# A one-core AdaLN, quantised FFN, GRU and expert-FFN kernel: where activations are transposed, how weight scales are found, and which PSUM bank the fill uses

## The chip, the cores and the metric

One NeuronCore of a Trainium2 chip runs the whole program. The metric is the device time of one execution in microseconds (us), lower is better. The figure for the kernel before is the median of three runs; beside it stands one profiled execution with its own time.

## The reference

x is [16, 256, 512] (batch, time, width). Everything below is computed in order:

```python
# layer 0, conditioning: block sums of x -> one attention over 8 blocks -> proj [B, 512]
xc = layernorm(x + proj) * gamma + beta
# layer 0, FFN: blocks of 32 share a power-of-two scale (MX quantisation) on both operands
gate, up = mx_linear(xc, w_gate), mx_linear(xc, w_up)      # 512 -> 2048
x = x + mx_linear(silu(gate) * up, w_down)                 # 2048 -> 512
# layer 1, conditioning: a GRU over the 256 time steps, h0 = cond_2048
gi, gh = x_t @ W_ih + b_ih, h @ W_hh + b_hh                # 512 -> 3 * 512
r, z = sigmoid(i_r + h_r), sigmoid(i_z + h_z)
n = tanh(i_n + r * h_n);  h = (1 - z) * n + z * h
# layer 1, FFN on the states hs: base product plus 16 rank-16 experts, the best 2 of 16 by a small router
out = x + hs @ W.T + bias + sum_e coeff_e * (hs @ A_e.T) @ B_e.T
```

## The kernel before

The 4096 rows (256 steps of 16 batch rows) are cut into 32 tiles of 128 rows, that is of 8 GRU steps. Each engine has its program written out by hand, with semaphores between them, so every engine works strictly in its own order.

Three stages follow each other. **The pieces** (0 to about 136 us): 24 weight pieces of 1024 columns are loaded, rounded to the quantised grid and turned into `wq`; beside them x is summed for the attention. **The fill** (about 136 to 244 us) and **the recurrence** are one software pipeline, run over a tile counter c = -4 ... 32 with 8 slots (s = 0 ... 7) each. In the slots of c the kernel does, for five different tiles at once: Q, the normalised and quantised input of tile c+4 (`qx`); F, the FFN of tile c+3; E, its end for tile c+2 (last `down` products, residual `x1`, and `x1T`); I, the GRU input products `x_wih` of tile c+1; R, the 8 recurrence steps of tile c, one a slot; L, the expert FFN of tile c-1. For c < 0 there is no R: that is the fill.

In slot (c, s) TensorE (PE in the profile) first does the 96 small products of the recurrence (L1305: `ps_rn`, then `ps_z`), which need the state `hT` of the slot before, and after them `others`: `gate` (even s, L1131) or `up` (odd s, L1137) of the FFN, transposes, `down` (L1155), `x_wih` (L1198), `base` and `route` (L1207). VectorE (DVE) does the chain of the recurrence from `r_half` (L747) to the low half of `hT` (L733), with other work before, within and after it. So a slot lasts as long as the longer of two things: PE's products of that slot, or the DVE chain that gives the next `hT`.

The FFN goes in four quarters n of 512 columns. For one quarter: `gate` into `ps_gate`, silu by ScalarE (ACT) into `gs`, `up` into the same bank (`ps_gate = ps_up`), `inter` = product by DVE (L827), block maxima, 8-bit value `f8`, clip `f8c` (L812), `qf` by GpSimd (POOL, L1020). Then `turn_inter` transposes `qf` with four PE transposes into PSUM (L1146), ACT copies it to `qfT` (L510), and `down` reads it a slot later. `qx` is turned once a tile in the same way (`turn_qx` L1186, copy L536 into `qxT`). PE does `turn_inter` in slots 0, 2, 4 and 6 and `turn_qx` in slot 7.

The GRU and expert weights are kept as two f16 parts with a power-of-two scale, from the largest absolute value. DVE finds these: for W_hh at (-3, 0) (`chunk_max`, L698), for W_ih at (-2, 0) (L662) and for WL (L667). W_ih is loaded into `wih` chunk by chunk once W_hh's parts have been taken from there: SP waits for `whh_lo` at (-3, 6). SP issues nearly all the DMAs, in order. In the fill `ps_z` lies idle.

## Time and profile before

| | us |
|---|---|
| median of 3 runs | 1749.04 (1748.38 to 1749.63) |
| the profiled execution's own time | 1750.32 |
| its span in the trace | 1748.5 |
| PE busy | 1585.6 (91%) |
| DVE busy | 1417.0 (81%) |
| ACT busy | 710.7 (41%) |
| POOL busy | 498.4 (29%) |
| DMA queue of the kernel's own transfers | 75.03 MB, 12.6% of 16 engines |

The span runs from 0; the pieces end at about 136 us, the first recurrence step starts at 244.4 us and the last at 1729.2 us. A busy share is the mean over stages with different limits, so it has to be read stage by stage; rows of the trace give start, duration, engine and line of one instruction or of a run of equal ones, and in brackets how long its engine had been idle and who ended that.

### The profile page before, as it was taken

How to read it: one execution, taken by the hardware profiler on the slowest of the kernel's cores; microseconds unless marked ns; L12 is line 12 of the kernel's file. 1: busy time of each engine (PE TensorE's matmuls, PEld its weight loads, DVE VectorE, ACT ScalarE, POOL GpSimd, SP SyncE). 2: the span in 40 equal slices, each digit the busy share in tenths (PEclk: the TensorE clock that was granted, in tenths of full speed). 3: DMA queues.
4: the chain of work that ended last, by engine and by line, in shares of the span. 5: the costliest groups of instructions: out<-in, count | busy, mean ns of one | idle time of the engine just before them, and what ended most of it. 6: DMA issues, size and time to landing. Idle time of an engine off the chain costs nothing.

```text
span 1748.5 us, 76340 instructions
## 1 busy us (share of the span) xinstructions
PE 1585.6 (91%) x32908; PEld 1240.8 (71%) x32908; DVE 1417.0 (81%) x5579; ACT 710.7 (41%) x1760; POOL 498.4 (29%) x573
## 2 busy tenths in 40 slices
PE   5534489999999999999999999999999999999986
PEld 2221167777787877778777777877777777778874
DVE  7898888888888888888888888888888888887654
ACT  5653244444444344434344434443443444443331
POOL 6773232222222222222222222222222222221100
PEclk9855699999999999999999999999999999999998
DMA  7733100011001010001111000110100010000000
GB/s 246 265 141 111 43 26 27 34 33 33 13 29 33 33 33 33 29 31 34 33 33 34 33 26 16 33 33 33 33 33 27 33 33 33 27 27 27 21 15 20
DMA packets 35408, 80.09 MB, mean 46 GB/s; under 512 B 4864, under 2 KB 5248, under 8 KB 34688
## 3 DMA queue, kind: packets, MB, share of 16 engines
q1 hardware_dynamic: 34784, 75.03, 12.6%
q8 instruction: 259, 4.24, 1.1%
q14 instruction: 77, 0.63, 0.1%
q10 hardware_dynamic: 288, 0.19, 0.0%
HBM read 58.43 MB, written 16.78 MB: 43 GB/s over the span
## 4 chain that ended last, share of the span: by engine, by line
PE 76%; DVE 16%; issue 2%; DMA 2%; POOL 2%; ACT 1%; DVEq 0%; ACTq 0%; POOLq 0%; SPq 0%
PE ps_rn_turn L1305 23%; PE ps_gi L1198 11%; PE ps_z L1305 10%; PE ps_gate_up L1137 6%; PE ps_down L1155 6%; PE ps_gate_up L1131 4%; PE ps_base L1207 4%; PE ps_base L1251 3%; PE ps_route L1207 3%; DVE fe L795 1%; PE ps_rn_turn L1146 1%; PE ps_rn_turn L1175 1%; DVE gi L595 1%; DVE gi L593 1%; DVE zn L780 1%
## 5 line engine op out<-in xcount | busy, mean ns | idle before, releaser
L1305 PE MATMUL ps_rn_turn<-hT,whh 128*128 128x32 f16 x16320 | 449.2, 176 | 39.2 <-DVE hT L733 38.8
L1305 PEld LDWEIGHTS ps_rn_turn<-hT,whh 128*128 128x128 f16 x16320 | 435.0, 96 | 65.7 <-DVE hT L733 58.2
L1020 POOL TENSOR_TENSOR qf<-f8c,fe 128x512 bf16<-128x512 bf16 x128 | 135.6, 1059 | 892.4 <-DVE f8c L812 872.8
L1198 PE MATMUL ps_gi<-x1T,wih 128*128 128x128 f16 x4608 | 288.6, 219 | 1.2 <-ACT gi L544 1.2
L1198 PEld LDWEIGHTS ps_gi<-x1T,wih 128*128 128x128 f16 x4608 | 270.3, 98 | 25.6 <-issue 1.5
L553 ACT ACTIVATE r_tanh<-r_pre,scale_half 128x64 f32<-128x64 f32 x256 | 89.0, 348 | 461.5 <-DVE r_pre L753 461.5
L1305 PE MATMUL ps_z<-hT,whh 128*128 128x32 f16 x8160 | 243.3, 176 | 0.0
L1305 PEld LDWEIGHTS ps_z<-hT,whh 128*128 128x128 f16 x8160 | 222.7, 96 | 0.0
L544 ACT ACTIVATE gi<-ps_gi,b_i,scale_x 128x128 f32<-128x128 f32 x384 | 144.7, 457 | 181.9 <-PE ps_gi L1198 181.9
L747 DVE TENSOR_TENSOR r_half<-ps_rn_turn,gi 128x64 f32<-128x64 f32 x256 | 56.6, 221 | 137.6 <-PE ps_rn_turn L1305 134.4
L555 ACT ACTIVATE z_tanh<-z_pre,scale_half 128x64 f32<-128x64 f32 x256 | 89.0, 348 | 157.9 <-DVE z_pre L763 157.9
L1131 PE MATMUL ps_gate_up<-wq,qxT 128*128 128x512 bf16 x512 | 135.5, 388 | 12.8 <-DVE inter L827 12.8
L1137 PE MATMUL ps_gate_up<-wq,qxT 128*128 128x512 bf16 x512 | 139.1, 396 | 2.4 <-ACT sg_gs L504 2.4
L1155 PE MATMUL ps_down<-wq,qfT 128*128 128x512 bf16 x512 | 134.4, 386 | 0.0
L557 ACT ACTIVATE n<-n_pre,scale_half 128x64 f32<-128x64 f32 x256 | 89.0, 348 | 20.6 <-DVE n_pre L770 10.5
L1207 PE MATMUL ps_base<-wl,hT 128*128 128x512 f16 x384 | 94.3, 382 | 0.0
L827 DVE TENSOR_TENSOR inter<-ps_gate_up,sg_gs 128x512 f32<-128x512 f32 x128 | 87.4, 683 | 7.1 <-PE ps_gate_up L1137 7.1
L504 ACT ACTIVATE sg_gs<-ps_gate_up 128x512 f32<-128x512 f32 x128 | 74.2, 580 | 44.5 <-PE ps_gate_up L1131 44.5
L788 DVE TENSOR_REDUCE fam<-inter 128x16 f32<-128x512 f32 x128 | 87.9, 686 | 4.4
L806 DVE SCALAR_TENSOR_TENSOR f<-inter,finv 128x512 fp8e4<-128x512 f32 x128 | 87.7, 685 | 0.0
L1155 PEld LDWEIGHTS ps_down<-wq,qfT 128*128 128x128 bf16 x512 | 48.6, 100 | 49.9 <-issue 4.6
L1137 PEld LDWEIGHTS ps_gate_up<-wq,qxT 128*128 128x128 bf16 x512 | 43.3, 99 | 55.6 <-issue 20.9
(197 smaller groups left out, 2590.1 us busy)
## 6 DMA issues: line engine op xcount, KB each, us to landing
wih<-in_x_steps SPq DMA_DIRECT2D x32, 256.0 KB, 5.4
xin<-in_x_steps SPq DMA_DIRECT2D x32, 256.0 KB, 3.5
xres<-in_x_steps SPq DMA_DIRECT2D x32, 256.0 KB, 3.1
x_dram<-x SPq DMA_DIRECT2D x32, 256.0 KB, 2.1
x_in<-x_dram SPq DMA_DIRECT2D x32, 256.0 KB, 2.8
out_rows<-y SPq DMA_DIRECT2D x32, 256.0 KB, 2.0
wst<-in_ffn_w SPq DMA_DIRECT2D x12, 512.0 KB, 3.7
sg_gs<-in_ffn_w SPq DMA_DIRECT2D x12, 512.0 KB, 3.9
```

Of the source, the lines that this page charges most:

```text
L544: last = nc.scalar.activation(gi_gate(i, g)[:, k, :], ps_gi[:, k * P:(k + 1) * P], ACT.Identity, bias=b_i[:, g * KD + k:g * KD + k + 1], s ...
L553: nc.scalar.activation(r_tanh[:, :], r_pre[:, :], ACT.Tanh, scale=HALF_S_INV).then_inc(r_ok, 1)
L555: nc.scalar.activation(z_tanh[:, :], z_pre[:, :], ACT.Tanh, scale=HALF_S_INV).then_inc(z_ok, 1)
L557: nc.scalar.activation(n[:, :], n_pre[:, :], ACT.Tanh, scale=HALF_S_INV).then_inc(n_ok, 1)
L788: v.tensor_reduce(am[:, :], blocked(src[:, :]), AX_X, ALU.max, apply_absolute_value=True).then_inc(small, 1)
L1020: g.tensor_tensor(blocked(qf[:, :]), blocked(f8c[:, :]), spread(fe16[:, :]), ALU.mult).then_inc(qf_done, 1)
L1131: last = mm(ps_gate[:, :], qxT[:, k, :], w_ffn(0, n, k), start=k == 0, stop=k == KD - 1)
L1137: last = mm(ps_up[:, :], qxT[:, k, :], w_ffn(8, n, k), start=k == 0, stop=k == KD - 1)
L1155: last = mm(ps_down[:, :], qfT[:, i, :], w_down(i), start=i == 0, stop=i == NF * KD - 1)
L1198: last = mm(ps_gi[:, j * P:(j + 1) * P], wih_parts[:, k, at:at + P], x1T[:, x, k, :], start=k + w + x == 0, stop=k == KD - 1 and w == 1)
L1207: last = mm(out, hT[l % 2][:, 2 * k + x, :], wl_parts[:, k, begin:begin + n], start=k + w + x == 0, stop=stop and w == 1)
L1305: last = mm(ps[:, (at + j) * 2 * B:(at + j + 1) * 2 * B], whh[:, k, u, gate * D + j * P:gate * D + (j + 1) * P], hx(t)[:, 2 * k:2 * k + 2, ...
```

## The change

1. `qx` and `qf` are no longer turned by PE and copied by ACT. SP issues `dma_start_transpose` from `qx` to `qxT` and from `qf` to `qfT`, in slots 7 and 1, 3, 5, 7. `qxT` has two buffers. POOL writes `qf` or `qx` again once that DMA has landed; `gate` and `down` wait for the landing.
2. The scales of W_hh, W_ih and WL come from row sums of absolute values, by ACT (`absolute_sums`), instead of maxima by DVE: W_hh's beside the last four pieces, W_ih's in slots 4 and 5 of c = -3, WL's in 6 and 7. In c = -3 and -2 ACT's `weights` come after `others`.
3. W_ih is loaded at (-3, 0), once the last piece is out, into tiles that are free by then (`wih_staged`: `gi` and the new `stage`); BT is loaded at (-1, 0).
4. The first 11 `up` products (`FILL_UPS`) go to `ps_z`, and `gs` has two buffers. `up` then waits for `inter` of the quarter before instead of silu, and `gate` no longer waits for `inter`.

The diff without its context lines and without the lists of semaphores; it is indented less:

```diff
@@ -67,6 +67,7 @@
+FILL_UPS = 11
@@ -114,8 +115,6 @@
-turn_b = ps_turn[:, :].bitcast(BF16)
-turn_q = ps_route[:, :].bitcast(BF16)
@@ -123,11 +122,12 @@
-wih, wl = sb("wih", [P, KD + 1, GATES]), sb("wl", [P, KD + 1, D + ROUTE])
+wih, wl = sb("wih", [P, KD, GATES]), sb("wl", [P, KD + 1, D + ROUTE])
-bt = sb("bt", [P, XA // P, D])
+stage = sb("stage", [P, 2 * GATES])
+bt = stage[:, 2 * PIECE:3 * PIECE].rearrange("p (m n) -> p m n", m=XA // P)
@@ -155,10 +155,10 @@
-qxT = sb("qxT", [P, KD, P], BF16)
+qxT = [sb(f"qxT{u}", [P, KD, P], BF16) for u in range(2)]
-gs, inter = sg_gs[:, D:2 * D], sb("inter", [P, D])
+gs, inter = [sg_gs[:, u * D:(u + 1) * D] for u in range(2)], sb("inter", [P, D])
@@ -179,7 +179,8 @@
-x1_in, x1_bias, y = sb("x1_in", [P, D]), sb("x1_bias", [P, D]), sb("y", [P, D])
+x1_in_bias, y = sb("x1_in_bias", [P, 2 * D]), sb("y", [P, D])
+x1_in, x1_bias = x1_in_bias[:, 0:D], x1_in_bias[:, D:2 * D]
@@ -191,10 +192,11 @@
-wst = [sb("wst0", [P, PIECE]), sg_gs[:, 0:PIECE]]
+wst = [stage[:, 0:PIECE], sg_gs[:, 0:PIECE]]
+wih_staged = [x[:, u * GATES:(u + 1) * GATES] for x in (gi, stage) for u in range(2)]
-w_abs = [sb(f"w_abs{u}", [P, PIECE], U8)[:, :] for u in range(2)]
+w_abs = [stage[:, PIECE + u * PIECE // 4:PIECE + (u + 1) * PIECE // 4].bitcast(U8) for u in range(2)]
@@ -215,7 +217,8 @@
-chunk_max, most = sb("chunk_max", [P, KD]), sb("most", [P, 2])
+row_sums, most = sb("row_sums", [P, 3, KD]), sb("most", [P, 2])
+unused = x1_in_bias[:, :].bitcast(BF16)
@@ -282,6 +285,10 @@
+def up_bank(i):
+    return ps_z if i < FILL_UPS else ps_up
@@ -378,16 +385,38 @@
+    def turn_qx(q):
+        sp.wait_ge(qx_done, count(q, 1, 1))
+        wait(sp, up_mm, count(q - 1, NF))
+        sp.dma_start_transpose(qxT[q % 2][:, :, :], qx[:, :]).then_inc(qx_turned[q % 2], 16)
+    def turn_inter(f, n):
+        sp.wait_ge(qf_done, count(f, NF, n + 1))
+        wait(sp, d_mm, count(f - 1, NF, n + 1))
+        sp.dma_start_transpose(qfT[:, n * KD:(n + 1) * KD, :], qf[:, :]).then_inc(qf_turned[n], 16)
+    def turns(c, s):
+        Q, F, E, I, R, L = stages(c)
+        if E and s == 1:
+            turn_inter(c + 2, NF - 1)
+        if Q and s == 7:
+            turn_qx(c + 4)
+        if F and s in (3, 5, 7):
+            turn_inter(c + 3, s // 2 - 1)
+        turns(c, s)
-        if c == -3 and s == STEPS - 2:
+        if (c, s) == (-3, 0):
+            sp.wait_ge(w_out, PIECES)
+            for k in range(KD):
+                sp.dma_start(wih_staged[k], W_ih[:, k, :]).then_inc(wih_loaded, 16)
-            for k in range(KD):
-                sp.wait_ge(whh_lo, min(k + 2, KD))
-                sp.dma_start(wih[:, k + 1, :], W_ih[:, k, :]).then_inc(wih_loaded, 16)
+        if (c, s) == (-1, 0):
+            sp.wait_ge(wih_lo, KD)
@@ -466,8 +495,21 @@
+    def absolute_sums(which, k, w):
+        wait(act, summed_w, which * KD + k)
+        nc.scalar.activation(unused[:, 0:w.shape[1]], w, ACT.Abs,
+                             accum_out=row_sums[:, which, k:k + 1]).then_inc(summed_w, 1)
+        if c == -3 and s in (4, 5):
+            for k in (2 * s - 8, 2 * s - 7):
+                act.wait_ge(wih_loaded, 16 * KD)
+                absolute_sums(1, k, wih_staged[k])
+        if c == -3 and s in (6, 7):
+            for k in (2 * s - 12, 2 * s - 11):
+                act.wait_ge(wl_loaded, 16)
+                absolute_sums(2, k, wl[:, k + 1, :])
@@ -481,8 +523,8 @@
-            wait(act, wih_lo, k)
-            nc.scalar.activation(wih_parts[:, k, 0:GATES], wih[:, k + 1, :], ACT.Copy,
+            act.wait_ge(whh_lo, KD)
+            nc.scalar.activation(wih_parts[:, k, 0:GATES], wih_staged[k], ACT.Copy,
@@ -500,16 +542,9 @@
-            wait(act, inter_done, count(f, NF, s // 2))
-            nc.scalar.activation(gs, ps_gate[:, :], ACT.Silu, scale=SHRUNK / W_GREW).then_inc(gs_done, 1)
-        for t, n, there in ((f, s // 2 - 2, F and s in (4, 6)), (e, s // 2 + 2, E and s in (0, 2))):
-            if there:
-                act.wait_ge(t_mm, count(t, NF, n + 1))
-                if n == 0:
-                    wait(act, d_mm, count(t, NF))
-                nc.scalar.activation(qfT[:, n * KD:(n + 1) * KD, :],
-                                     turn_b[:, 0:D].rearrange("p (k n) -> p k n", k=KD),
-                                     ACT.Copy).then_inc(t_ev, 1)
+            at = count(f, NF, s // 2)
+            wait(act, inter_done, at - 1)
+            nc.scalar.activation(gs[at % 2], ps_gate[:, :], ACT.Silu, scale=SHRUNK / W_GREW).then_inc(gs_done, 1)
@@ -530,11 +565,6 @@
-        if Q and s == 7:
-            act.wait_ge(q_mm, count(c + 4, 1, 1))
-            wait(act, up_mm, count(c + 4, NF))
-            nc.scalar.activation(qxT[:, :, :], turn_q[:, 0:D].rearrange("p (k n) -> p k n", k=KD),
-                                 ACT.Copy).then_inc(q_ev, 1)
@@ -555,13 +585,18 @@
-        if c in (-3, -2, 0):
+        if c == 0:
+        if c in (-3, -2):
+            weights(c, s)
+        if p >= PIECES - KD:
+            act.wait_ge(whh_loaded, 16 * KD)
+            absolute_sums(0, p - PIECES + KD, wih[:, p - PIECES + KD, :])
@@ -655,17 +690,12 @@
-        at = 2 * KD + 9
+        at = 9
-            for k in range(KD):
-                dve.wait_ge(wih_loaded, 16 * KD)
-                v.tensor_reduce(chunk_max[:, k:k + 1], wih[:, k + 1, :], AX_X, ALU.max,
-                                apply_absolute_value=True).then_inc(most_dve, 1)
-            dve.wait_ge(most_dve, at)
-            v.reduce_max(most[:, 0:1], chunk_max[:, :], AX_X).then_inc(most_dve, 1)
-            dve.wait_ge(wl_loaded, 16)
-            v.tensor_reduce(most[:, 1:2], wl[:, 1:KD + 1, :].rearrange("p k n -> p (k n)"), AX_X, ALU.max,
-                            apply_absolute_value=True).then_inc(most_dve, 1)
+            dve.wait_ge(most_mm, 1)
+            dve.wait_ge(summed_w, 3 * KD)
+            for i in range(2):
+                v.reduce_max(most[:, i:i + 1], row_sums[:, i + 1, :], AX_X).then_inc(most_dve, 1)
@@ -681,7 +711,7 @@
-            v.scalar_tensor_tensor(wih_parts[:, k, GATES:2 * GATES], wih[:, k + 1, :], S_I,
+            v.scalar_tensor_tensor(wih_parts[:, k, GATES:2 * GATES], wih_staged[k], S_I,
@@ -693,21 +723,17 @@
-            for k in range(KD):
-                dve.wait_ge(whh_loaded, 16 * KD)
-                v.tensor_reduce(chunk_max[:, k:k + 1], wih[:, k, :], AX_X, ALU.max,
-                                apply_absolute_value=True).then_inc(most_dve, 1)
-            dve.wait_ge(most_dve, KD)
-            v.reduce_max(most[:, 0:1], chunk_max[:, :], AX_X).then_inc(most_dve, 1)
+            dve.wait_ge(summed_w, KD)
+            v.reduce_max(most[:, 0:1], row_sums[:, 0, :], AX_X).then_inc(most_dve, 1)
-            scales_in_row(s, KD + 2, least, scale_row)
+            scales_in_row(s, 2, least, scale_row)
-            dve.wait_ge(most_dve, KD + 8)
+            dve.wait_ge(most_dve, 8)
@@ -824,7 +850,7 @@
-                v.tensor_tensor(inter[:, :], ps_up[:, :], gs, ALU.mult).then_inc(inter_done, 1)
+                v.tensor_tensor(inter[:, :], up_bank(at)[:, :], gs[at % 2], ALU.mult).then_inc(inter_done, 1)
@@ -1016,7 +1042,7 @@
-                wait(pool, t_mm, at)
+                wait(pool, qf_turned[(at - 1) % NF], (at + NF - 1) // NF * 16)
@@ -1048,7 +1074,7 @@
-            wait(pool, q_mm, count(q, 1))
+            wait(pool, qx_turned[(q - 1) % 2], (q + 1) // 2 * 16)
@@ -1125,29 +1151,27 @@
-            pe.wait_ge(q_ev, count(f, 1, 1))
-        wait(pe, inter_done, count(f, NF, n))
+            pe.wait_ge(qx_turned[f % 2], (f // 2 + 1) * 16)
+        i = count(f, NF, n)
+        wait(pe, gs_done, i)
+        if i > FILL_UPS:
+            pe.wait_ge(inter_done, i)
-            last = mm(ps_gate[:, :], qxT[:, k, :], w_ffn(0, n, k), start=k == 0, stop=k == KD - 1)
+            last = mm(ps_gate[:, :], qxT[f % 2][:, k, :], w_ffn(0, n, k), start=k == 0, stop=k == KD - 1)
-        pe.wait_ge(gs_done, count(f, NF, n + 1))
+        i = count(f, NF, n)
+        if i < FILL_UPS:
+            wait(pe, inter_done, i)
+        else:
+            pe.wait_ge(gs_done, i + 1)
-            last = mm(ps_up[:, :], qxT[:, k, :], w_ffn(8, n, k), start=k == 0, stop=k == KD - 1)
+            last = mm(up_bank(i)[:, :], qxT[f % 2][:, k, :], w_ffn(8, n, k), start=k == 0, stop=k == KD - 1)
-    def turn_inter(f, n):
-        pe.wait_ge(qf_done, count(f, NF, n + 1))
-        if n == 2:
-            wait(pe, x_ev, count(f, 1))
-        wait(pe, t_ev, count(f, NF, n))
-        for k in range(KD):
-            last = turn_(turn_b[:, k * P:(k + 1) * P], qf[:, k * P:(k + 1) * P], idb[:, :])
-        last.then_inc(t_mm, 1)
-        pe.wait_ge(t_ev, count(f, NF, n + 1))
+        pe.wait_ge(qf_turned[n], (f + 1) * 16)
@@ -1170,21 +1194,11 @@
-        pe.wait_ge(t_ev, count(e + 1, NF, 2))
+        pe.wait_ge(x1_done, count(e, 1, 1))
+        wait(pe, x_ev, count(e, 1))
-    def turn_qx(q, E, L):
-        pe.wait_ge(qx_done, count(q, 1, 1))
-        wait(pe, q_ev, count(q, 1))
-        if E:
-            pe.wait_ge(x_scale_ok, count(q - 2, 1, 1))
-        elif L:
-            pe.wait_ge(wxaT_ok, count(q - 5, 1, 1))
-        for k in range(KD):
-            last = turn_(turn_q[:, k * P:(k + 1) * P], qx[:, k * P:(k + 1) * P], idb[:, :])
-        last.then_inc(q_mm, 1)
@@ -1213,7 +1227,6 @@
-            wait(pe, q_ev, count(l + 4, 1, 1))
@@ -1276,10 +1289,6 @@
-        if E and s in (0, 2):
-            turn_inter(e, s // 2 + 2)
-        if F and s in (4, 6):
-            turn_inter(f, s // 2 - 2)
@@ -1288,8 +1297,6 @@
-        if Q and s == 7:
-            turn_qx(c + 4, E, L)
@@ -1310,10 +1317,9 @@
-        at = (c + 3) * (KD + 9)
+        at = 0 if c == -3 else 9
-            pe.wait_ge(most_dve, at + KD + 2)
-            pe.wait_ge(q_ev, c + 4)
+            pe.wait_ge(most_dve, at + 2)
@@ -1321,7 +1327,7 @@
-            pe.wait_ge(most_dve, KD + 9 if c == -3 else 2 * KD + 20)
+            pe.wait_ge(most_dve, 9 if c == -3 else 20)
@@ -1337,6 +1343,8 @@
+        if (c, s) == (-1, 7):
+            pe.wait_ge(inter_done, FILL_UPS)
```

## Rows read from the trace of the kernel before

**Rows 1.** The page, part 4: the chain that ended last, shares by engine.
```profile
PE 76%; DVE 16%; issue 2%; DMA 2%; POOL 2%; ACT 1%; DVEq 0%; ACTq 0%; POOLq 0%; SPq 0%
```

**Rows 2.** Tile hT: recurrence group, then min/median/max ns, first and last start.
```profile
L1305 PE MATMUL ps_rn_turn<-hT,whh x16320: 176/176/210, 249.5 to 1730.8; 128*128 128x32 f16 x200
```

**Rows 3.** Timeline of PE: starts of slots 7, 0, 1, 3, 5, 0.
```profile
709.98 1.75 PE L1305 MATMUL ps_rn_turn<-hT,whh 128*128 128x32 f16 x64
...
716.78 1.75 PE L1305 MATMUL ps_rn_turn<-hT,whh 128*128 128x32 f16 x64
...
722.57 1.78 PE L1305 MATMUL ps_rn_turn<-hT,whh 128*128 128x32 f16 x64
...
734.43 1.77 PE L1305 MATMUL ps_rn_turn<-hT,whh 128*128 128x32 f16 x64 [0.59 <-DVE hT L733]
...
745.81 1.75 PE L1305 MATMUL ps_rn_turn<-hT,whh 128*128 128x32 f16 x64
...
763.97 1.75 PE L1305 MATMUL ps_rn_turn<-hT,whh 128*128 128x32 f16 x64
```

**Rows 4.** Timeline of DVE, same stretch: ends of chains, and one slow small operation.
```profile
709.20 0.22 DVE L733 TENSOR_TENSOR hT<-h,hT 128x64 f16<-128x64 f32 x1
...
714.59 0.23 DVE L733 TENSOR_TENSOR hT<-h,hT 128x64 f16<-128x64 f32 x1
...
721.58 0.22 DVE L733 TENSOR_TENSOR hT<-h,hT 128x64 f16<-128x64 f32 x1
...
731.07 0.88 DVE L795 TENSOR_SCALAR fe<-fam 128x16 f32<-128x16 f32 x1
...
745.48 0.22 DVE L733 TENSOR_TENSOR hT<-h,hT 128x64 f16<-128x64 f32 x1
```

**Rows 5.** The chain of waits, in order of time: start, us, group.
```profile
716.72 0.22 PE ps_route L1186 x4
...
720.21 0.22 PE ps_rn_turn L1146 x4
```

**Rows 6.** Timeline of POOL: two quarters of qf in a steady tile.
```profile
700.34 1.05 POOL L1020 TENSOR_TENSOR qf<-f8c,fe 128x512 bf16<-128x512 bf16 x1 [9.67 <-DVE f8c L812]
...
710.64 1.05 POOL L1020 TENSOR_TENSOR qf<-f8c,fe 128x512 bf16<-128x512 bf16 x1 [4.76 <-DVE f8c L812]
```

**Rows 7.** The DMA view: issues by tile, KB each, median us to landing.
```profile
wih<-in_x_steps SPq DMA_DIRECT2D x32, 256.0 KB, 5.4
...
out_rows<-y SPq DMA_DIRECT2D x32, 256.0 KB, 2.0
...
beta_b<-in_beta SPq DMA_DIRECT2D x1, 256.0 KB, 8.8
```

**Rows 8.** Timeline of DVE in the fill.
```profile
136.13 6.72 DVE L698 TENSOR_REDUCE chunk_max<-wih 128x1 f32<-128x1536 f32 x4
...
148.79 0.69 DVE L827 TENSOR_TENSOR inter<-ps_gate_up,sg_gs 128x512 f32<-128x512 f32 x1 [2.94 <-PE ps_gate_up L1137]
...
176.23 6.73 DVE L662 TENSOR_REDUCE chunk_max<-wih 128x1 f32<-128x1536 f32 x4 [2.45 <-DMA wih<-in_W_ih]
...
183.07 3.61 DVE L667 TENSOR_REDUCE most<-wl 128x1 f32<-128x3328 f32 x1
...
231.18 0.69 DVE L827 TENSOR_TENSOR inter<-ps_gate_up,sg_gs 128x512 f32<-128x512 f32 x1 [0.79 <-PE ps_gate_up L1137]
...
237.84 0.69 DVE L827 TENSOR_TENSOR inter<-ps_gate_up,sg_gs 128x512 f32<-128x512 f32 x1 [0.72 <-PE ps_gate_up L1137]
```

**Rows 9.** Timeline of POOL in the fill: the first qx.
```profile
136.29 1.05 POOL L1052 TENSOR_TENSOR qx<-q8c,qe 128x512 bf16<-128x512 bf16 x1 [1.50 <-DVE q8c L812]
```

**Rows 10.** Timeline of PE in the fill: the first gate, and the first recurrence step.
```profile
144.22 1.89 PE L1131 MATMUL ps_gate_up<-wq,qxT 128*128 128x512 bf16 x4
...
244.42 1.75 PE L1305 MATMUL ps_rn_turn<-hx_first,whh 128*128 128x32 f16 x64
```

**Rows 11.** Timeline of ACT in the fill: two copies of 1536 columns.
```profile
151.96 3.03 ACT L480 ACTIVATE whh<-wih,scale 128x1536 f16<-128x1536 f32 x2
```

6 lines of the change are left out of this document (3 added, 3 removed).

## The prediction

> **What bounds the kernel now.** I read the chain of waits first: of the chain that ended last, PE has 76% and DVE 16% [rows 1]. That is a mean over stages, so the next view is the timeline by stage. Recurrence steps follow each other from 244.42 us on [rows 10], and their last group starts at 1730.8 [rows 2]; before that lie the pieces and the fill.
>
> *Recurrence.* A tile of 8 slots takes 763.97 - 716.78 = 47.19 us [rows 3]. For each slot the reader compares two rows: when `hT` is complete (start plus duration of L733) and when PE starts the next slot's products. If PE starts later, PE's own work sets the slot and the difference is DVE's slack. If PE shows idle time ended by `hT`, the DVE chain sets it. Slack before slot 7: 709.98 - 709.42 = 0.56; before slot 0: 716.78 - 714.82 = 1.96; before slot 1: 722.57 - 721.80 = 0.77; before slot 5: 745.81 - 745.70 = 0.11, of which about 0.05 is the signal's way. Slot 3 begins after 0.59 us of idleness that `hT` ended [rows 3, 4]. So six or seven of the eight slots are PE's, and slot 2 is DVE's: its chain holds a `fe` of 0.88 us on 16 columns [rows 4].
>
> *Fill.* DVE works nearly without a gap, and two blocks stand out: 6.72 us of W_hh maxima, and 2.45 us waiting for W_ih followed by 6.73 and 3.61 us of maxima [rows 8].
>
> **The change, part by part.**
>
> *Turns in the recurrence.* Each group of four PE transposes takes 0.22 us of the chain [rows 5]. A tile loses five: slots 0, 2, 4, 6 and 7, 1.10 us of PE. What remains of each is read from the slack behind it:
> - slot 0: slack 0.77 is more than 0.22, so 0.22 is kept.
> - slot 2: PE already waits 0.59, so 0.
> - slot 4: only 0.11 - 0.05 = 0.06 can be kept; then `hT` is late, and DVE goes on without a gap into slot 5, so perhaps nothing.
> - slot 6: slack 0.56, 0.22 kept. Slot 7: slack 1.96, 0.22 kept.
>
> Sum 0.66 to 0.72; I take 0.70. F and Q both run beside the recurrence in c = 0 to 27, 28 tiles: **19.6 us**. The ACT copies that go were never waited for by the chain of `hT` beyond 1% [rows 1]; I give them 0.
>
> *What takes the turns' place.* A DMA must land before `down` (two slots later, about 12 us) and before POOL writes the single `qf` again. The tighter one is `qf`: its shortest gap is 710.64 - 701.39 = 9.25 us [rows 6]. No row shows a transposing DMA. The nearest are plain DMAs of 256 KB, twice these bytes: 2.0, 5.4 and 8.8 us from issue to landing [rows 7]. I take 5.4, the slower of the two that occur 32 times, because a transpose of 2-byte elements should go worse than a copy; both ends stay for the range. All three are below 9.25, so it is hidden in the recurrence, at cost 0. If that cover is gone, the price is in the last rival.
>
> SP waits in order, so each `turn_inter` holds up what is queued behind it. In slot 7 that is the store of x1 and of y, which waits for `y` of the same slot anyway; in slot 3 the load of `xin`, which POOL needs only in the next tile. Cost 0.
>
> The Trainium skill speaks against this part. VectorE: DVE Perf Modes, section The three transpose paths, gives a 128x128 bf16 transpose as 390 ns on TensorE and 1309 ns by DMA, and its rules say to use TensorE where PSUM will do. The trace has PE at 0.22 us for four. By the page four blocks by DMA would be 5.2 us, an estimate; hidden or not decides, and the sum would stay as it is.
>
> *Start of the fill.* The block of 6.72 leaves DVE. In its place ACT does four sums of 1536 columns between the last pieces, 3.03 / 2 = 1.5 us each by its copies [rows 11], and an activation with a sum may take a little more. ACT is in the round of the pieces (DVE waits for its squares), and it has 1 to 3.5 us free in each: I let one of the four delay the last pieces, 1.5 us. The first `qx` is then ready at 136.29 + 1.05 + 1.5 = 138.8 [rows 9], and with 5.4 for its DMA the first `gate` starts at 144.2, where it starts now, 144.22 [rows 10]. So **the 6.7 us buy nothing by themselves**: the wait for the maxima is replaced by a wait for a DMA. With 2.0 it would be 3.4 us earlier, with 8.8 3.4 later. The free bank gives the first `up` the 0.7 us for which it waited on silu, and in c = -3 ACT's sums before the W_hh copies cost DVE about as much (0.8). Together **0**.
>
> *Middle of the fill.* W_ih is issued about 23 us earlier and has long landed; ACT's eight sums (4 x 1.5 for W_ih, 4 x about 0.9 for WL by width) fit into c = -3 by about 168 us, before DVE needs them. Gone are 2.45 + 6.73 + 3.61 = 12.8 us [rows 8], come are two maxima over four columns, 0.3: **12.5 us**. Since all behind hangs on DVE's order, it passes through.
>
> *End of the fill, c = -1.* DVE waits twice for `up`, 0.79 and 0.72 [rows 8]. `gate` no longer waits for `inter` and a turn is gone, PE comes some 1.7 us earlier, and DVE becomes the bound: 1.5, plus the last turn before the first step, 0.2: **1.7 us**. The pairs of quarters are only 6 to 7 us apart here; DMAs beyond about 6 us would take this back.
>
> *Sum.* 19.6 + 0 + 12.5 + 1.7 = 33.8 us. Against the profiled execution: span 1748.5 - 33.8 = 1714.7, its own time 1750.3 - 33.8 = 1716.5. It stood 1.3 us above the median, so the median becomes 1749.0 - 33.8 = **1715.2 us**. Bounds of the unknown costs: the first landing +-3.4, later ones up to +3, ACT beside the pieces -1.5 to +3 (none or all but one delayed), slot 4 +-1.
>
> **Rivals.**
> 1. *PE's time isn't given back in the recurrence.* DVE, busy 81%, becomes the bound in more slots than I read, or `qf` and `hT` shift so that other small operations get as slow as the `fe` of 0.88. For it: slack of 0.11 before slot 5. Against: 0.56 to 1.96 elsewhere. Then only the fill gains, 14.2 us: 1735.
> 2. *More comes.* Transposes land in 2 us (3.4 earlier at the start, another 1 to 2 in c = -3), and slots 2 and 4 keep their 0.22 too because ACT without its copies shortens DVE's chain: 28 x 1.10 = 30.8 instead of 19.6. Both: 1749.0 - 30.8 - 14.2 - 4 = 1700.
> 3. *Slower: the DMA takes longer than the gap.* `qf` is one buffer: write (1.05), signal (about 0.4), DMA, next write. Once the DMA needs L, a tile takes at least 4 x (1.45 + L). It reaches 47.19 at L = 10.3; from L = 10.5 the loss over 29 tiles eats the 14.2 us of the fill, and at L = 12 a tile is 53.8, which is 29 x 6.6 = 191 us more: about 1926. For it: a landing of 8.8 for a DMA with nothing to transpose, and five such DMAs a tile in one queue. Against: half the bytes, and DMA engines nearly idle here.
> 4. *It doesn't do what it says*: PE is not the bound and the fill is bound by something that the removed blocks hid; within 0.2% of before. Rows 3 and 8 speak against it.
>
> **How the numbers follow.** Forecast (about 1706 to 1726) 0.60; rival 1 0.17; rival 2 0.12; rival 3 0.08; rival 4 0.03. The range leaves out rivals 3 and 4 and the far part of 2: 1702 to 1736. Faster 0.60 + 0.17 + 0.12 = 0.89; within 0.2% (3.5 us, about what a measurement of this kernel can tell from no change) 0.03; slower 0.08.
>
> **What would show it.** Tile period about 46.5 us instead of 47.19, with PE idle before slot 3 near 0.8 and a first idle before slot 5. Landings of the transposing DMAs between 2 and 9 us, and POOL's `qf` still released by DVE's `f8c`, not by a DMA. First `gate` near 144, released by a DMA. No DVE wait or maxima around 176; the first recurrence step near 230. Wrong would make it: a DMA as what POOL or `down` waits for in the recurrence, ACT stretching the last pieces by more than 3 us, or tables reloaded by ACT between its sums and silu.

## The result, and the profile after

The changed kernel takes 1716.51 us (median of four runs, 1716.04 to 1720.65) against 1749.34 (1748.38 to 1751.13) for the kernel before: ratio 0.9814, 95% interval 0.9802 to 0.9826. Predicted were 1715.2 us, in a range of 1702 to 1736. Inside the sum, though, the landing of the DMA and the free bank had a wrong size, and a new wait in the fill was missed. In the experiments "the changed kernel" is this one; on another chip it took 1717.86 us.

The profiled execution was the longest of the four, 1720.65 us, with a span of 1718.8: it lies 4.1 us above the forecast for a profiled execution (1716.5), where the median lies 1.3 above its own. Where its 29.7 us against the span before came from, by the starts of DVE's `inter` (the product of silu and up; they are numbered from 0), of the first recurrence step and of the last:

| stretch | before | after | difference | predicted |
|---|---|---|---|---|
| to inter 0: pieces, start of the fill | 148.79 | 146.17 | -2.6 | 0 |
| inter 0 to inter 6: middle of the fill | 62.30 | 48.76 | -13.5 | -12.5 |
| inter 6 to inter 7 | 9.44 | 12.26 | +2.8 | 0 |
| inter 7 to the first step | 23.89 | 22.77 | -1.1 | -1.7 |
| first step to the start of the last | 1484.8 | 1469.2 | -15.6 | -19.6 |
| behind it | 19.3 | 19.6 | +0.3 | 0 |

The page of the changed kernel, lines of its parts 1, 3 and 4: busy time, the DMA queue of the kernel's own transfers, and the chain that ended last by engine (before: [rows 1]).

```profile
PE 1556.5 (91%) x32268; PEld 1204.4 (70%) x32268; DVE 1393.3 (81%) x5571; ACT 644.6 (38%) x1624; POOL 497.5 (29%) x573
...
q1 hardware_dynamic: 121824, 96.02, 20.9%
...
PE 76%; DVE 15%; issue 3%; ACT 2%; DMA 2%; POOL 2%; SPq 0%; DVEq 0%; ACTq 0%; POOLq 0%
```

PE lost 29 us of work and DVE 24, and the queue moved 96 MB instead of 75, in 121824 packets instead of 34784. The shares of the chain are nearly the same as before: they don't tell where the gain is. The timeline does.

**Recurrence.** PE of the changed kernel, starts of slots 7, 0, 1, 3, 5, 0 and of the last slot of all (before: [rows 3]):

```profile
690.69 1.75 PE L1312 MATMUL ps_rn_turn<-hT,whh 128*128 128x32 f16 x64
697.26 1.75 PE L1312 MATMUL ps_rn_turn<-hT,whh 128*128 128x32 f16 x64
702.83 1.77 PE L1312 MATMUL ps_rn_turn<-hT,whh 128*128 128x32 f16 x64
...
714.69 1.76 PE L1312 MATMUL ps_rn_turn<-hT,whh 128*128 128x32 f16 x64 [0.81 <-DVE hT L759]
...
726.01 1.77 PE L1312 MATMUL ps_rn_turn<-hT,whh 128*128 128x32 f16 x64
...
728.53 0.22 PE L1187 MATMUL ps_route<-idb,row_power 128*1 128x128 bf16 x1
...
743.75 1.75 PE L1312 MATMUL ps_rn_turn<-hT,whh 128*128 128x32 f16 x64
...
1699.18 1.75 PE L1312 MATMUL ps_rn_turn<-hT,whh 128*128 128x32 f16 x64
```

DVE beside it (before: [rows 4]), the transposing DMAs in the view of DMA issues (last number: median us to landing), and POOL's `qf` ([rows 6]):

```profile
711.32 0.88 DVE L821 TENSOR_SCALAR fe<-fam 128x16 f32<-128x16 f32 x1
...
725.73 0.22 DVE L759 TENSOR_TENSOR hT<-h,hT 128x64 f16<-128x64 f32 x1
...
728.32 0.16 DVE L910 TENSOR_SCALAR row_power<-row_max 128x1 uint16<-128x1 uint16 x1
```
```profile
qfT<-qf SPq DMA_TRANSPOSE x128, 2.5
...
qxT<-qx SPq DMA_TRANSPOSE x32, 2.9
```
```profile
715.84 1.05 POOL L1046 TENSOR_TENSOR qf<-f8c,fe 128x512 bf16<-128x512 bf16 x1 [3.67 <-DVE f8c L838]
```

A tile takes 743.75 - 697.26 = 46.49 us, 0.70 less. Slots 6, 7 and 0 became 0.22, 0.23 and 0.23 shorter (medians of 27 tiles), slot 4 by 0.06. Slot 2 is DVE's still: PE's wait ahead of slot 3 grew from 0.59 to 0.81 and took what the missing turn gave. In slot 5, longer by 0.04, PE now comes so early that its one small product on `row_power` waits for DVE: 728.32 + 0.16 is 728.48, and it starts at 728.53. POOL's `qf` waits for DVE's `f8c` in all 128 cases, never for a transpose, which lands in 2.5 us (median) and not in the 5.4 of the prediction.

**Start of the fill.** DVE, PE and SP of the changed kernel:

```profile
140.98 0.16 DVE L727 TENSOR_REDUCE most<-row_sums 128x1 f32<-128x4 f32 x1 [2.29 <-ACT x_in_bias L500]
...
146.17 0.69 DVE L853 TENSOR_TENSOR inter<-ps_z,sg_gs 128x512 f32<-128x512 f32 x1 [2.17 <-PE ps_z L1170]
```
```profile
141.41 1.01 PE L1326 MATMUL ps_route<-idf,most 128*1 128x128 f32 x4 [2.98 <-DVE most L729]
142.43 1.89 PE L1160 MATMUL ps_gate_up<-wq,qxT 128*128 128x512 bf16 x4
```
```profile
139.85 1.31 SPq L391 DMA_TRANSPOSE qxT<-qx  x1
```

And a row of the kernel before, PE, which the prediction had not read; it stands just ahead of its first gate in [rows 10]:

```profile
143.27 1.01 PE L1320 MATMUL ps_route<-idf,most 128*1 128x128 f32 x4 [5.27 <-DVE most L703]
```

The turn of `most` comes before the first gate in PE's order. Before, PE stood idle for 5.27 us ahead of it, for DVE's maxima. In the changed kernel two things end within 0.04 us of each other: the DMA of `qx`, issued at 139.85, lands at 142.38, and the turn of `most`, for which PE waits 2.98 us because DVE waits 2.29 for ACT's fourth sum, ends at 142.42. The gate starts at 142.43.

How much of the 2.6 us is the change's needs more than these two traces. The eleven traces of kernels with the sums beside the pieces start `q8c`, DVE's last step before the first `qx`, anywhere from 132.99 to 138.85 us (the changed kernel: 138.27 and 137.69), the three without them at 135.56 to 136.28. Behind `q8c` the traces agree: from there to inter 0 it takes 12.8 to 13.0 us in the three kernels with W_hh's maxima on DVE, and 7.5 to 8.2 in the ten with the sums and two banks. So about 5 us are gained behind the pieces, and this execution lost 2.5 of them ahead of it.

**Middle and end of the fill.** DVE of the changed kernel, and ACT at its second wait (before: [rows 8]):

```profile
177.67 0.69 DVE L853 TENSOR_TENSOR inter<-ps_z,sg_gs 128x512 f32<-128x512 f32 x1 [2.62 <-PE ps_z L1170]
...
199.66 1.82 DVE L714 SCALAR_TENSOR_TENSOR wih<-stage,scale_l,wih 128x1536 f16<-128x1536 f32 x1 [2.73 <-ACT wih L527]
...
206.52 0.75 DVE L955 SCALAR_TENSOR_TENSOR x1T<-ps_rn_turn,scale_x,x1T 128x512 f16<-128x512 f32 x1 [3.68 <-ACT x1T L566]
...
223.60 0.69 DVE L853 TENSOR_TENSOR inter<-ps_z,sg_gs 128x512 f32<-128x512 f32 x1 [0.72 <-PE ps_z L1170]
```
```profile
197.49 0.60 ACT L547 ACTIVATE sg_gs<-ps_gate_up 128x512 f32<-128x512 f32 x1 [11.05 <-PE ps_gate_up L1160]
197.98 1.56 ACT L527 ACTIVATE wih<-stage,scale_l 128x1536 f16<-128x1536 f32 x1
```

The blocks of [rows 8] at 176 and 183 us are gone. In their place stands a new wait of 2.73 us: the fourth high part of W_ih stands in ACT's order behind a silu, which waits for a gate, and DVE waits for the high part. Of the two waits for `up` in c = -1, 0.79 and 0.72, one is gone and one is left. The first step starts at 229.96 instead of 244.42, 14.5 us earlier.

### The profile page after: what moved, and what is told of

It is laid out like the page before. It is cut to its first block, busy times and chain, and to the rows that moved or that the text cites. A ratio compares the mean times of both kernels' runs of the same rounds, so it can differ in the third digit from the quotient of the medians.

```text
span 1718.8 us, 75109 instructions
## 1 busy us (share of the span) xinstructions
PE 1556.5 (91%) x32268; PEld 1204.4 (70%) x32268; DVE 1393.3 (81%) x5571; ACT 644.6 (38%) x1624; POOL 497.5 (29%) x573
## 3 DMA queue, kind: packets, MB, share of 16 engines
q1 hardware_dynamic: 121824, 96.02, 20.9%
## 4 chain that ended last, share of the span: by engine, by line
PE 76%; DVE 15%; issue 3%; ACT 2%; DMA 2%; POOL 2%; SPq 0%; DVEq 0%; ACTq 0%; POOLq 0%
PE ps_rn_turn L1312 24%; PE ps_gi L1212 12%; PE ps_z L1312 10%; PE ps_down L1179 6%; PE ps_gate_up L1170 6%; PE ps_base L1221 4%; PE ps_gate_up L1160 4%; PE ps_base L1264 3%; PE ps_route L1221 3%; DVE fe L821 1%; POOL qfT L1028 1%; DVE gi L630 1%; DVE gi L628 1%; PE ps_rn_turn L1200 1%; DVE zn L806 1%
## 5 line engine op out<-in xcount | busy, mean ns | idle before, releaser
L1212 PEld LDWEIGHTS ps_gi<-x1T,wih 128*128 128x128 f16 x4608 | 274.5, 98 | 38.2 <-issue 3.8
L1179 PE MATMUL ps_down<-wq,qfT 128*128 128x512 bf16 x512 | 138.0, 394 | 0.0
L1160 PE MATMUL ps_gate_up<-wq,qxT 128*128 128x512 bf16 x512 | 133.0, 382 | 0.0
L1170 PE MATMUL ps_gate_up<-wq,qxT 128*128 128x512 bf16 x468 | 123.6, 387 | 0.5 <-ACT sg_gs L547 0.5
L587 ACT ACTIVATE n<-n_pre,scale_half 128x64 f32<-128x64 f32 x256 | 89.0, 348 | 21.0 <-DVE n_pre L796 11.2
L853 DVE TENSOR_TENSOR inter<-ps_gate_up,sg_gs 128x512 f32<-128x512 f32 x117 | 79.7, 681 | 0.0
L1056 POOL TENSOR_TENSOR xg<-xn,gamma_b 128x512 f32<-128x512 f32 x32 | 40.8, 1276 | 119.2 <-DVE xn L936 119.2
```

The source lines that it names most:

```text
L587: nc.scalar.activation(n[:, :], n_pre[:, :], ACT.Tanh, scale=HALF_S_INV).then_inc(n_ok, 1)
L1160: last = mm(ps_gate[:, :], qxT[f % 2][:, k, :], w_ffn(0, n, k), start=k == 0, stop=k == KD - 1)
L1170: last = mm(up_bank(i)[:, :], qxT[f % 2][:, k, :], w_ffn(8, n, k), start=k == 0, stop=k == KD - 1)
L1179: last = mm(ps_down[:, :], qfT[:, i, :], w_down(i), start=i == 0, stop=i == NF * KD - 1)
L1212: last = mm(ps_gi[:, j * P:(j + 1) * P], wih_parts[:, k, at:at + P], x1T[:, x, k, :], start=k + w + x == 0, stop=k == KD - 1 and w == 1)
```

## Experiments

Each kernel differs from the changed kernel by the edit shown, unless its text says otherwise. A ratio is to runs of the kernel before on the same chip.

### One part of the change undone, or done alone

**The turns back on PE** (loads, sums and the bank stay as changed):

```diff
-            def turn_qx(q):
...
-                sp.dma_start_transpose(qxT[q % 2][:, :, :], qx[:, :]).then_inc(qx_turned[q % 2], 16)
...
+            def turn_inter(f, n):
+                pe.wait_ge(qf_done, count(f, NF, n + 1))
...
+                for k in range(KD):
+                    last = turn_(turn_b[:, k * P:(k + 1) * P], qf[:, k * P:(k + 1) * P], idb[:, :])
```

> The changed kernel with part 1 undone: PE turns qx and qf again and ACT copies them, everything else stays changed. My theory: the turns are worth 0.71 us a tile in 28 tiles of the recurrence, 19.9 us, and nothing in the fill but the last turn, 0.2. So 1716.5 + 20.1 = 1736.6 us, tile period 47.19, first recurrence step about 230.2 us. Rival (the gain is mostly the fill's, and the turns gave back what they saved): 1717 to 1722 us.

**The turns alone** (the kernel before, with its turns by DMA and nothing else of the change):

```diff
+            def turn_inter(f, n):
...
+                sp.dma_start_transpose(qfT[:, n * KD:(n + 1) * KD, :], qf[:, :]).then_inc(qf_turned[n], 16)
...
-                for k in range(KD):
-                    last = turn_(turn_b[:, k * P:(k + 1) * P], qf[:, k * P:(k + 1) * P], idb[:, :])
```

> The kernel before with part 1 alone: qx and qf turned by DMA, maxima by DVE, W_ih late, one bank. My theory: the parts add, so 1749.3 - 20.1 = 1729.2 us, tile period 46.48, first step at about 244.2 us. Rival (the parts need each other: without the second bank the DMA landing shows in the fill, 2.5 us for each of the 12 quarters of the fill): 1729 + up to 20 us.

With PE's turns: 1738.43 us, ratio 0.9943 (0.9928 to 0.9958), 1.8 us above the expectation, which the interval of 5 us does not tell apart. The turns alone: 1738.34 us, ratio 0.9936 (0.9921 to 0.9951), that is 9 us slower than expected, a miss. The tile period is as expected in both, 47.19 and 46.49 us. In the fill both lose. From inter 0 to the first step it takes 88.35 us with PE's turns (changed kernel 83.79), and 99.73 with the turns alone (before 95.63). With PE's turns that does not show in the first step, 229.07 for 230.2 expected, because inter 0 came at 140.72, 5.4 us before that of the changed kernel; 5.3 of these lie before `q8c`, that is before anything is turned. DVE and ACT with PE's turns:

```profile
153.14 1.82 DVE L746 SCALAR_TENSOR_TENSOR whh<-wih,scale,whh 128x1536 f16<-128x1536 f32 x1 [1.14 <-ACT whh L504]
```
```profile
147.91 0.60 ACT L535 ACTIVATE qfT<-ps_rn_turn 128x512 bf16<-128x512 bf16 x1 [3.58 <-PE ps_rn_turn L1174]
```

ACT's copies of the turned quarters share its order with the eight sums and the high parts of W_hh, and DVE waits for these three times, 1.14, 1.05 and 0.86 us. DVE and SP with the turns alone:

```profile
182.81 6.74 DVE L667 TENSOR_REDUCE chunk_max<-wih 128x1 f32<-128x1536 f32 x4 [8.49 <-DMA wih<-in_W_ih]
```
```profile
166.72 1.20 SPq L387 DMA_TRANSPOSE qfT<-qf  x1
...
168.59 2.76 SPq L408 DMA_DIRECT2D wih<-in_W_ih  x4
```

SP waits in order. It stands in the turn of a quarter until 166.72, so the late load of W_ih, issued at 161.82 before, is issued at 168.59, and DVE waits for it for 8.49 us where it waited for 2.45 [rows 8]; from the first issue to the last landing the four loads take 14.2 us here and 14.4 before. The early load takes W_ih out of that place. So the parts don't add: 10.4 us for the turns alone, 10.3 for all the rest, 32 for both. Of the 11 us between, the stretch from inter 0 to the first step holds 8.6 (4.1 lost with the turns alone, 7.3 gained by the rest, 11.8 by both). The others aren't assigned: the pieces alone differ by several us from one execution to the next.

**One bank in the fill:**

```diff
-FILL_UPS = 11
+FILL_UPS = 0
...
-                    pe.wait_ge(inter_done, FILL_UPS)
+                    wait(pe, inter_done, FILL_UPS)
```

> The changed kernel itself again, unaltered, as the measure for the three kernels run beside it on the same chip. Expected 1716.5 us, 32 to 33 us under the kernel before (ratio 0.981). Also asked of it: whether its recurrence again holds slots at the half clock. The profiled execution of the changed kernel had six such slots, some 7.6 us in all, where the kernel before had three; if they come with the turn's removal (a longer wait of TensorE ahead of slot 3, 0.82 us where it was 0.59), this execution has some again, in other steps; if they were an accident of that one execution, it has as few as the kernel before.

> The changed kernel without the last part of the change: the up products go to the one bank in the fill as everywhere else. Two theories. Mine: in the fill, gate and up of the next piece no longer run ahead of the product of the two, so each of the eleven turns in which VectorE waits for silu and up loses its own start-up again (a wait of 0.6 to 0.8 us per turn where it is exposed, some four of them); 1719 us, 2 to 3 us above the changed kernel. The rival: the second bank hides behind VectorE, which is the bound of the middle of the fill, and taking it away costs nothing (1716.5). A third: the products of gate and up queue behind the late product in order and the loss runs on from turn to turn, up to 0.8 x 11 = 9 us (1725).

The changed kernel again: 1717.86 us, ratio 0.9814 (0.9794 to 0.9834). With one bank: 1729.06 us, ratio 0.9881 (0.9865 to 0.9897). All three theories missed: it is 11.2 us, and not in small waits turn by turn. DVE and ACT with one bank:

```profile
163.37 1.82 DVE L751 SCALAR_TENSOR_TENSOR whh<-wih,scale,whh 128x1536 f16<-128x1536 f32 x1 [5.70 <-ACT whh L522]
...
176.82 1.82 DVE L751 SCALAR_TENSOR_TENSOR whh<-wih,scale,whh 128x1536 f16<-128x1536 f32 x1 [4.88 <-ACT whh L522]
```
```profile
158.14 0.60 ACT L547 ACTIVATE sg_gs<-ps_gate_up 128x512 f32<-128x512 f32 x1 [6.67 <-PE ps_gate_up L1160]
158.64 1.48 ACT L500 ACTIVATE x_in_bias<-gi 128x1536 bf16<-128x1536 f32 x1
160.01 0.19 ACT L500 ACTIVATION_READ_ACCUMULATOR x_in_bias<-gi 128x1 f32 x1
...
161.78 1.56 ACT L522 ACTIVATE whh<-wih,scale 128x1536 f16<-128x1536 f32 x1
```

It is a ring of three engines. The next gate waits for `inter`, which in one bank must have been read. ACT's silu waits for that gate; behind the silu stand two sums and the high part; DVE waits for the high part, and its next `inter` stands behind. With two banks the gate, and with it silu and all that is behind it, runs ahead of `inter`, and the sums lie in time that DVE needs anyway. In this order of ACT, its work for the weights is cheap only because of the bank. DVE waits 11.6 us in three waits for W_hh's high parts with one bank, and 0.79 us in one with two. The change puts two things behind silu, the sums and the high parts themselves (`weights` after `others`); no run has one bank without the one or the other, so how the 11.2 us divide between them is open.

**W_hh's maxima back on DVE, no sums beside the last pieces:**

```diff
-                if p >= PIECES - KD:
-                    act.wait_ge(whh_loaded, 16 * KD)
-                    absolute_sums(0, p - PIECES + KD, wih[:, p - PIECES + KD, :])
...
+                    for k in range(KD):
...
+                        v.tensor_reduce(row_sums[:, 0, k:k + 1], wih[:, k, :], AX_X, ALU.max,
+                                        apply_absolute_value=True).then_inc(summed_w, 1)
...
                     v.reduce_max(most[:, 0:1], row_sums[:, 0, :], AX_X)
```

> The changed kernel with the four maxima of W_hh's rows taken by VectorE at the start of the fill, as in the kernel before (6.7 us there), and no sums of them on ScalarE beside the last four pieces. It computes the scales of W_hh from maxima as the kernel before does. My theory, that the 6.7 us taken from VectorE at this place buy next to nothing because the first gate product waits for something else: VectorE's start of the fill comes 1.5 us earlier without ScalarE's sums in the pieces, then takes 6.7 us more, and the first gate moves by 0 to 2.5 us; 1716 to 1719 us. The rival, that VectorE sets the start of the fill by then and all of it returns: 1716.5 + 6.7 - 1.5 - 2.3 (its wait for the fourth sum) = 1719.4 at the least and 1723 at the most.

1717.71 us, ratio 0.9816 (0.9801 to 0.9832): no difference to the changed kernel beside it. Its trace is not the same, though. DVE and PE:

```profile
135.90 6.72 DVE L725 TENSOR_REDUCE row_sums<-wih 128x1 f32<-128x1536 f32 x4
```
```profile
143.09 1.01 PE L1327 MATMUL ps_route<-idf,most 128*1 128x128 f32 x4 [7.37 <-DVE most L730]
144.03 1.89 PE L1161 MATMUL ps_gate_up<-wq,qxT 128*128 128x512 bf16 x4
```

Against the changed kernel in its own execution on this chip, `q8c` comes 2.1 us earlier (135.56 for 137.69), the maxima 2.25 later, the first gate 2.2 later (144.03 for 141.85), inter 0 2.8 later and the first step 3.05 later. Here the DMA of `qx` has landed more than 4 us before the gate, so the maxima alone hold it. In these two executions 1.3 us of it came back in the recurrence and 1.5 behind it, by slots at the half clock (below) and a tail that was not followed further. From `q8c` to inter 0 it takes 12.80 us for 7.89: that is what moving W_hh's maxima takes out of the fill. What ACT's four sums cost beside the pieces in return, 1.5 us by the prediction, isn't settled: 2.1 by this pair, 0.7 in the mean of all the traces, and kernels that are the same up to there differ by 4.5 us. So 3 to 4 us remain by the rows, and the times, with intervals of 5 and 7 us, neither show nor exclude it.

**W_ih's and WL's maxima back on DVE, the load still early:**

```diff
-                    for k in (2 * s - 8, 2 * s - 7):
...
-                        absolute_sums(1, k, wih_staged[k])
...
+                    for which, ws in ((1, wih_staged), (2, [wl[:, k + 1, :] for k in range(KD)])):
+                        for k in range(KD):
+                            v.tensor_reduce(row_sums[:, which, k:k + 1], ws[k], AX_X, ALU.max,
+                                            apply_absolute_value=True).then_inc(summed_w, 1)
```

> The changed kernel with the maxima of W_ih and WL back on VectorE in the second stage of the fill (6.7 + 3.6 us as in the kernel before), while W_ih is still loaded early. The scales of these weights come from maxima again. It tells apart how much of the middle of the fill came from the early load and how much from VectorE's relief. My theory: the 10.3 us return nearly in full, because VectorE is the bound there; less 0.3 us for the maxima of the sums and less up to 2.5 us in which VectorE waits anyway (for x1T 3.7 us, for the high parts 2.7 us): +7.5 to +10 us, 1724 to 1727 us. The rival, the early load alone was worth it and VectorE's work hides in its waits: 1717 to 1720 us.

1726.41 us, ratio 0.9872 (0.9856 to 0.9889), against 0.9814: 0.0058 x 1749 = 10.1 us. My theory held at its upper end, the rival fell. DVE:

```profile
169.43 3.40 DVE L692 TENSOR_REDUCE row_sums<-gi 128x1 f32<-128x1536 f32 x2
172.75 3.40 DVE L692 TENSOR_REDUCE row_sums<-stage 128x1 f32<-128x1536 f32 x2
176.07 3.79 DVE L692 TENSOR_REDUCE row_sums<-wl 128x1 f32<-128x832 f32 x4
```

10.4 us of DVE work (169.43 to 179.86) without a wait ahead of it, and the stretch from inter 0 to the first step is 93.99 us, 10.2 more than in the changed kernel. The middle of the fill is DVE's, and its work there counts in full.

### How slow a transpose may be

Further transposes of the same quarter go ahead of the real one, each waited for. REPEAT is 3, 4 and 5:

```diff
...
+                for r, spare in enumerate(scratch):
+                    sp.dma_start_transpose(spare[:, :, :], qf[:, :]).then_inc(qf_turned[n], 16)
+                    sp.wait_ge(qf_turned[n], (f * REPEAT + r + 1) * 16)
                 sp.dma_start_transpose(qfT[:, n * KD:(n + 1) * KD, :], qf[:, :]).then_inc(qf_turned[n], 16)
...
```

> The changed kernel with each transpose of a quarter made long: two further transposing DMAs of the same data into unused tiles go ahead of the real one, each waited for by the queue before the next is issued. They add work and leave none out. One transpose lands 2.5 us after its issue, so three in a chain take about 3 x 2.6 = 7.8 us. The theory of the prediction (rival 3): beside the recurrence a transpose is free until 4 x (1.45 + L) passes the length of a tile, that is up to L of 10.2; at 7.8 the tile period stays at 46.5 us. In the fill quarters follow each other in as little as 4.7 us, and there a gap of 1.45 + 7.8 = 9.3 us for each of ten makes it 15 to 20 us longer: about 1735 us in all. The rival: the slack of the two-slot distance is smaller than that and the period already grows, by 1 us or more (1765 us and above).

> The same with three further transposes ahead of the real one: L about 4 x 2.6 = 10.4 us, right at the point from which the prediction's rival 3 becomes decisive. By its formula, 4 x (1.45 + 10.4) = 47.4 us a tile, 0.9 more than 46.5; over 29 tiles 26 us, and the fill longer by 30 us: about 1772 us. If the shortest of the four gaps (10.3 us from one qf to the next) can't be made up by the three longer ones, the period is 46.5 + (11.9 - 10.3) = 48.1 us and the time 1794 us.

> The same with four further transposes: L about 13 us. By the formula of the prediction's rival 3 a tile takes 4 x (1.45 + 13) = 57.8 us, 11.3 more than 46.5, over 29 tiles 328 us, and the fill 45 us more: about 2090 us. If the tile period stays near 47 the formula is wrong and the transposes overlap in some way that I don't see.

One execution each. Three: 1735.6 us, tile period 46.48 us, the stretch from inter 0 to the first step 19.8 us longer than in the changed kernel: as expected, and the period can't tell it from one transpose, though 8 of the `qf` of the recurrence already wait for the DMA. Four: 1913.0 us, mean period 51.6 (expected 47.4 to 48.1). Five: 2248.7 us, mean period 62.5 (expected 57.8). POOL with three, and with four:

```profile
709.58 1.05 POOL L1051 TENSOR_TENSOR qf<-f8c,fe 128x512 bf16<-128x512 bf16 x1 [4.72 <-DVE f8c L843]
```
```profile
717.12 1.05 POOL L1051 TENSOR_TENSOR qf<-f8c,fe 128x512 bf16<-128x512 bf16 x1 [10.62 <-DMA qfT<-qf]
```

With four, POOL waits for the DMA in 127 of 128 cases, as rival 3 said. Both terms of the formula 4 x (1.45 + L) can be read in the traces. From the end of a `qf` to the landing of the last link it takes 8.9 us in the mean with three, 11.7 with four and 14.4 with five, over the tiles of the recurrence: 2.9 us a link and not the 2.6 that I had put in, because a link lands 2.5 us after its issue in the median but part of them need 3 to 4. And write and signals take 1.05 + 0.03 + 0.13 = 1.21 us, not 1.45. 4 x (1.21 + 11.68) = 51.6 is the period that was measured; the miss is L, too small by 1.3 and 1.4 us, less 0.24 for the signals. The mean granted clock is lower too, 0.929 with four and 0.960 in the changed kernel, but with POOL's quarters following each other by the DMA alone it does not set the period.

### Two additions

**ACT's high parts of W_ih ahead of its other work in c = -2**, against the new wait of 2.73 us:

```diff
-                if c == 0:
+                if c in (-2, 0):
                     weights(c, s)
                 others(c, s, Q, F, E, I, L)
-                if c in (-3, -2):
+                if c == -3:
                     weights(c, s)
```

> The changed kernel, but ACT does the high parts of W_ih in c = -2 ahead of its other work of the slot, as before the change; c = -3 stays changed. In the changed kernel the fourth high part comes behind a silu that waits for a gate which waits for DVE's row_power, and DVE idles 2.73 us for it. My theory: these 2.7 us lie on the path to the first step, so 1713.8 us and first step near 227.3. Rival: DVE only comes to its next wait (x1T, 3.68 us) earlier and waits longer there: 1716.5 us.

1711.39 us, ratio 0.9792 (0.9779 to 0.9806). The wait is gone, and from inter 0 to the first step it takes 81.08 us for 83.79: 2.7 less, as expected. The other 2.4 us under the 1713.8 is not from the edit by any row I found: in this execution inter 0 came at 143.84 for 146.17, and the recurrence, whose code and slots are the same, held fewer slots at the half clock.

**`xn` one place earlier on DVE beside the recurrence**, against the `fe` of 0.88 us:

```diff
-                if Q and here == (2, 0):
+                if Q and here == ((1, 3) if c >= 0 else (2, 0)):
```

> The changed kernel, with DVE's xn (one operation of 0.54 us) moved ahead of inter and its maxima, for c >= 0, so that POOL's two xg run 1.3 us earlier and are done before DVE's fe of slot 2. My theory: fe of 0.88 us is slow because POOL's xg runs beside it; alone it takes 0.17. Slot 2 is the one slot that DVE sets, so it falls from 5.69 to about 4.98: 28 x 0.7 = 19.6 us, 1697 us, and PE's idle before slot 3 falls from 0.82 to about 0.1. Rival (the slow fe has another cause, or the slowness moves to the next small operation of the same chain): 1716 us, tile period 46.48.

1696.76 us, ratio 0.9695 (0.9679 to 0.9712). The theory held: slot 2 takes 4.97 us for 5.69, a tile 45.78. POOL and DVE of the changed kernel, then of this one:

```profile
710.90 1.27 POOL L1058 TENSOR_TENSOR xg<-xg,beta_b 128x512 f32<-128x512 f32 x1
```
```profile
700.59 1.28 POOL L1058 TENSOR_TENSOR xg<-xg,beta_b 128x512 f32<-128x512 f32 x1
```
```profile
702.33 0.17 DVE L821 TENSOR_SCALAR fe<-fam 128x16 f32<-128x16 f32 x1
```

In the changed kernel `fe` (711.32 to 712.20) lies beside POOL's `xg` (710.90 to 712.17) and ends with it. Here `xg` has ended at 701.87 before `fe` starts, and `fe` takes 0.17. The Trainium skill, SBUF — State Buffer, section SBUF: two separate sides, says of the port pair that VectorE and GpSimd share that whoever starts first holds it for its whole instruction and the other is blocked; of VectorE's operations it names those in a 2-port mode and those with two inputs in SBUF. The rows agree: `fe` starts 0.42 us behind `xg` and ends 0.03 us behind it, and so it is in all 27 tiles from the second on. An operation that reads PSUM isn't slowed: this one of the changed kernel lies beside the same `xg` and takes what it takes elsewhere:

```profile
711.19 0.21 DVE L782 TENSOR_TENSOR hn<-ps_rn_turn,hn_half 128x64 f32<-128x64 f32 x1
```

**Both:**

> Both of my additions in one kernel: ScalarE's weight work ahead of the other work in the fill's second stage, and the normalised x one place earlier on VectorE beside the recurrence. Alone the second gave 1696.8 us, and the first took 2.7 us from the stretch between the first product of silu and up and the first step of the recurrence. They touch different stretches, so they should add: 1696.8 - 2.7 = 1694 us (ratio 0.969 to the kernel before). If the fill's gain was an accident of how early its pieces ran, this gives 1696.8 again.

1693.18 us, ratio 0.9685 (0.9666 to 0.9703), 0.8 us from the expectation. From inter 0 to the first step 81.01 us, a tile 45.79: each part is where it was alone. It has the lowest median of the kernels here; its interval overlaps that of `xn` alone.

## Why the prediction was right, and where it was not

**Turns in the recurrence: right, slot by slot.** 0.70 a tile was predicted by comparing two rows in each slot, and 0.70 to 0.71 was measured. The 19.6 us came out as 15.6 in the profiled execution and 17.4 in the second one, and as 17.5 to 20.0 in the five other kernels with transposes by DMA and the same tile period. The rest is PE's clock, a term that the sum did not have: over the 28 tiles the slots of the changed kernel are together 4.8 and 3.2 us longer than their medians, those of the kernel before 1.3. Two slots of the changed kernel's PE and the view of windows (stretch, length, then busy time of PE, PEld, DVE, ACT, POOL, granted clock as a share of 2.4 GHz, DMA share, GB/s):

```profile
341.41 1.76 PE L1312 MATMUL ps_rn_turn<-hT,whh 128*128 128x32 f16 x64 [1.16 <-DVE hT L759]
...
343.86 1.87 PE L1170 MATMUL ps_gate_up<-wq,qxT 128*128 128x512 bf16 x4
```
```profile
341.40:348.60 7.20, 7.19 (x130) 5.14 (x131) 5.93 (x21) 1.04 (x3) 2.27 (x2) 0.76 0.25 57
...
714.70:720.60 5.90, 5.90 (x131) 4.74 (x132) 4.71 (x18) 1.04 (x3) 2.28 (x2) 1.00 0.24 36
```

The same slot in two tiles: 7.2 us at a mean granted clock of 0.76 (part of it at 0.50, that is 1.2 GHz, with `up` at 1.87 us where it takes 1.02), and 5.9 us at 1.00. Ahead of the slow one PE had waited 1.16 us for `hT`, ahead of the other 0.81. Slot 3 of tile 2 in all the traces but those of the chains of four and five:

| kernel | wait ahead of it, us | length, us |
|---|---|---|
| changed kernel, twice; chain of three | 1.16 | 7.20 to 7.24 |
| weights first; one bank | 1.16 | 5.91 |
| maxima of W_hh by DVE; PE's turns | 0.90 to 0.94 | 5.90 to 5.91 |
| before; turns alone; maxima of W_ih by DVE | 0.60 to 0.81 | 5.90 to 5.91 |
| `xn` earlier; both additions | 0.45 | 5.90 to 5.91 |

In this slot the clock fell only behind the longest wait, and not always behind that one; in tile 14 it fell once behind 0.89. Without the turn each wait ahead of slot 3 is 0.22 longer. Whether this makes such slots more frequent is open: two traces with the longest wait had none here, and no run set the wait by itself.

**Transposing DMAs: hidden, as predicted, by a wider margin.** 2.5 us for 5.4 assumed. I took the nearest plain DMA and leaned to the slow side; the rows had 2.0 for one of them. VectorE: DVE Perf Modes, section The three transpose paths, in the Trainium skill, gives 1309 ns for one 128x128 block, which would be 5.2 us for four, an estimate; the trace has 1.19 us of SP's queue to issue four and 2.5 us until they have landed. Its advice to use PE where PSUM will do did not hold for this kernel: the DMA's time is hidden and PE's is not.

**Start of the fill: right as a mechanism, wrong in size, 2.6 us for 0.** "The wait for the maxima is replaced by a wait for a DMA" holds: the first gate starts as that DMA has landed. The term that was mis-sized is the landing, 5.4 us for 2.5 measured. The pieces ended 2.5 us later than before where 1.5 was assumed, and 144.2 - 2.9 + 1.0 = 142.3 is the gate as it came, 142.43. With 5.4 us it could not have started before 139.85 + 5.4 = 145.2, later than before. "The 6.7 us buy nothing by themselves" hung on the slow landing: with a fast one they are worth about 5 us behind the pieces, less what the sums cost there. The prediction also missed a second path to the same gate, ACT's fourth sum, `most` and its turn. It ends 0.04 us behind the landing, so the 3.4 us that were to come with a landing of 2.0 would not have come.

**Middle of the fill: right in size, 12.5 for 13.5, but 2.8 went back.** The 12.8 us of wait and maxima passed through to the time, as the kernel with W_ih's maxima on DVE shows (10.1 us). What was missed is what is late next: ACT's high part behind silu, 2.73 us. With the high parts ahead of silu it is gone, and the time from inter 6 to inter 7 is 9.45 us again. "All behind hangs on DVE's order" is true only as long as no other engine's order is in it.

**The free bank: mis-priced.** The prediction gave it 0.7 us at the start and most of 1.5 at the end. Taken away it costs 11.2 us, because ACT's sums and high parts, which the same change puts behind silu, then wait for each gate with it. Right was that `gate` no longer waits for `inter`; wrong was to price it by waits of the kernel before, in which ACT had nothing to do there.

**End of the fill: 1.1 for 1.7.** One of the two waits for `up` stayed, 0.72. PE of the changed kernel ahead of that `up`:

```profile
222.31 0.22 PE L1187 MATMUL ps_route<-idb,row_power 128*1 128x128 bf16 x1 [0.41 <-DVE row_power L910]
222.46 1.04 PE L1170 MATMUL ps_z<-wq,qxT 128*128 128x512 bf16 x4
```

It stands behind a small product on `row_power`, which DVE gives only at 222.26. In the kernel before it is the same: `row_power` done at 236.49, the product at 236.54, `up` behind it. Neither a free bank nor a missing turn changes that wait.

**The rivals.** 1 (PE's time not given back) fell by the slots' lengths. 2 (more comes) was right on the landing and wrong on slots 2 and 4. 3 was right as a mechanism and as a formula; the landing of 2.5 us is a quarter of the 10.3 from which it decides. That the median came within 1.3 us is partly luck: in the profiled execution -2.6 and -1 in the fill stand against +2.8 and +0.6 there and +4 in the recurrence, and its sum is off by 4.1 us.

## What to carry to other kernels

Before a block of work is called free, read the row of the consumer itself, and who ended its idle time: an in-order engine waits for what stands ahead in its order as well as for what the next operation needs. Where a wait is replaced by another, look for a third that ends at the same time. Parts of a change that meet in one engine's order have no price of their own (10.4 + 10.3 us alone, 32 together; a free bank worth 11 us once the engine behind it had more to do). And a slot's slack, the end of one chain against the start of the next work, forecasts a change of a few tenths of a us well enough to be multiplied by the number of tiles.

## What the hardware showed

- A DMA that transposes 128x512 elements of 2 bytes within SBUF keeps SP's queue for 1.19 us and lands 2.4 us after its issue at the least (median 2.5, up to 4.5). In chains of four and five it takes 2.9 us a link in the mean. 160 of them added 21 MB and 87000 packets to the queue's count.
- An activation that also sums its row takes a second instruction of 0.19 us behind the 1.48 us of the 1536 columns.
- A VectorE `tensor_scalar` on 16 columns in SBUF takes 0.17 us, and 0.88 when it starts beside an elementwise operation of GpSimd on 512 columns: in 27 of 27 tiles it ends 0.03 us behind it. A VectorE operation that reads PSUM takes 0.21 us beside the same one as elsewhere. The slow one cost 0.7 us a tile, 20 us in all.
- TensorE's granted clock fell to the half within slots that followed a wait of about 1 us, in the same slot in three traces and not in two others with the same wait; such a slot was 1.2 to 1.6 us longer than its median in the changed kernel.
